# Storing the output of a macaron transformer layer from inside its last feed-forward loop, in 32 pieces, and not after it in 8

## The reference

```python
def ffn(x, U1, V1, b1, U2, V2, b2):      # 1024 -> 256 -> 4096 -> 256 -> 1024
    P = x @ U1
    H = gelu(P @ V1 + b1)
    Q = H @ U2
    return Q @ V2 + b2
def attn(x, ...):                        # 16 heads of 64, causal softmax, output projection
    ...
x = x + 0.5 * ffn(layernorm(x), U1, V1, b1, U2, V2, b2)
x = x + attn(layernorm(x), ...)
x = x + 0.5 * ffn(layernorm(x), U1, V1, b1, U2, V2, b2)
return x
```

## Time and profile before

| what | value |
|---|---|
| median of 3 runs | 2022.56 us (2018.89 to 2022.8) |
| the profiled execution, its own time | 2016.72 us |
| span of its slowest core (core 5), first to last instruction | 2015.2 us |
| spans of the eight cores | 1970.7 to 2015.2 us |
| PE busy on core 5 | 1566.1 us, 78% of the span |
| DVE, ACT busy | 28%, 28% |
| DMA traffic | 72.69 MB, mean 36 GB/s |
| granted clock of PE on core 5 | 0.752 of full speed on average |

### The profile page before, as it was taken

The page is one execution under the profiler, slowest core; times in us unless marked ns, Lnnn a source line. Parts: engine busy times, 40 slices in busy tenths (PEclk is TensorE's granted clock), DMA queues, the critical chain, the costliest instruction groups (busy, mean ns, idle before and its releaser), DMA issues. The chain is left out here.

```text
span 2015.2 us, 17883 instructions; the slowest of 8 cores (1970.7 to 2015.2 us)
## 1 busy us (share of the span) xinstructions
PE 1566.1 (78%) x5640; PEld 417.8 (21%) x5640; DVE 566.7 (28%) x947; ACT 557.2 (28%) x615; POOL 105.6 (5%) x117
## 2 busy tenths in 40 slices
PE   2389999547659879697797986969878794799994
PEld 0022222112212112121121221212211230222220
DVE  2522211752321413314133141231411236221111
ACT  1232232200013333333333333333444103222320
POOL 0100000000000001000010000100000101000000
PEclk7598899769866858678585685876865895878976
DMA  8400000300130010200102001010000125000004
GB/s 249 128 0 0 1 0 1 105 21 32 32 73 1 11 43 0 53 1 11 42 1 53 1 11 43 0 42 1 0 22 0 52 61 180 1 0 0 1 0 167
DMA packets 70984, 72.69 MB, mean 36 GB/s; under 512 B 20551, under 2 KB 59607, under 8 KB 68846
## 3 DMA queue, kind: packets, MB, share of 16 engines
q1 hardware_dynamic: 70894, 71.54, 12.4%
HBM read 50.49 MB, written 12.58 MB: 31 GB/s over the span
## 5 line engine op out<-in xcount | busy, mean ns | idle before, releaser
L725 ACT ACTIVATE pt<-p_big 128x1024 bf16<-128x1024 f32 (+3 forms) x320 | 286.5, 895 | 584.6 <-PE p_big L686 328.4
L680 PE MATMUL p_big<-qgA,kgA 65*128 65x512 bf16 (+3 forms) x320 | 147.5, 461 | 128.5 <-ACT pt L725 67.8
L570 ACT ACTIVATE hb<-p_big 128x1024 bf16<-128x1024 f32 x128 | 130.9, 1024 | 329.4 <-PE p_big L493 325.1
L491 PE MATMUL p_big<-pb,v1b 128*128 128x512 bf16 x512 | 164.8, 406 | 15.7 <-DVE pb L528 15.7
L639 PE MATMUL p_big<-pt,v_pair 128*64 128x512 bf16 (+3 forms) x320 | 155.3, 485 | 0.0
L642 PE MATMUL p_big<-pt,v_pair 128*64 128x512 bf16 (+3 forms) x320 | 154.6, 483 | 0.0
L686 PE MATMUL p_big<-qgB,kgB 65*128 65x512 bf16 (+3 forms) x320 | 153.8, 481 | 0.0
L635 PE MATMUL p_big<-pt,ones_bf 128*1 128x512 bf16 (+3 forms) x320 | 152.2, 476 | 0.0
L631 PE MATMUL p_big<-pt,ones_bf 128*1 128x512 bf16 (+3 forms) x320 | 143.9, 450 | 0.3
L501 PE MATMUL p_big<-hb,u2b 128*128 128x512 bf16 x512 | 139.3, 397 | 4.7 <-ACT hb L570 4.7
L230 PE MATMUL p_big<-xb_s,ones_bf 128*1 128x512 bf16 x96 | 50.8, 529 | 77.0 <-DVE xb_s L251 76.8
(11 more groups left out here) (149 smaller groups left out, 1604.2 us busy)
## 6 DMA issues: line engine op xcount, KB each, us to landing
wstage<-u SPq DMA_DIRECT2D x40, 256.0 KB, 4.9
wstage<-v SPq DMA_DIRECT2D x40, 256.0 KB, 4.5
x<-xT SPq DMA_DIRECT2D x8, 1024.0 KB, 11.1
outT<-x SPq DMA_DIRECT2D x8, 1024.0 KB, 10.2
wstage<-vw SPq DMA_DIRECT2D x16, 256.0 KB
vscr<-vb_s SPq DMA_DIRECT2D x32, 128.0 KB
v_pair<-vscr SPq DMA_DIRECT2D x8, 512.0 KB
wst<-ow SPq DMA_DIRECT2D x8, 512.0 KB, 4.2
```

The costliest lines, as they stand in the source:

```text
L491: tensor.matmul(psl, v1b[:, rc, 128 * fc:128 * (fc + 1)], pb[:, c % 2, rc, :], start=(rc == 0), stop=False)
L570: ACT.inc(scalar.activation(hb[:, 2 * (fp % 2):2 * (fp % 2) + 2, :], psl.rearrange("p (a b) -> p a b", a=2), AF.Gelu_apprx_tanh))
L680: mm = tensor.matmul(p_big[:, 0:w], kgA[:, ksl], qgA[:, lo:hi], start=True, stop=not first)
L725: ch["XA"].inc(scalar.activation(pt[:, :, i % 2, 0:w], p_big[:, 0:1024].rearrange("p (a b) -> p a b", a=2)[:, :, 0:w], AF.Exp))
```

## The change

The stores move into the main block of `f2`. SP gets a stream there: for each chunk and each `xadd` it waits until VectorE has done that `xadd`, and issues two DMAs, one for each feature block, of 128 partitions by 512 tokens (256 KB; 2 KB for each partition, to rows of `outT` that are 8 KB apart). The eight stores of 1 MB after the block are gone. In their place stands a block in which ScalarE waits for the semaphore of all stores. The sublayer `f1` is built as before.

```diff
                     pos = {ev: fp0 + i + 1 for i, ev in enumerate(plan)}
                     dpos = {ev: ws0 + i + 1 for i, ev in enumerate(dplan)}
+
+                    if tag == "f2":
+                        @blk.sync
+                        def _(sync):
+                            for c in range(NTC):
+                                for dp in range(4):
+                                    sync.wait_ge(EV.h, dpos[("xadd", c, dp)])
+                                    for f in (2 * dp, 2 * dp + 1):
+                                        ST.inc(sync.dma_start(
+                                            d_out.ap()[128 * f:128 * (f + 1),
+                                                       512 * c:512 * (c + 1)],
+                                            x[:, f, 512 * c:512 * (c + 1)]), 16)
...
         if PHASES >= 3:
             emit_ffn_sublayer("f2")
 
-        emit_dump_fm(d_out, x)
+        with nc.Block() as blk:
+            @blk.scalar
+            def _(scalar):
+                scalar.wait_ge(ST.h, ST.v)
```

## The result

| | before | after |
|---|---|---|
| median, 16 runs each | 2019.19 us (2011.54 to 2028.86) | 1996.51 us (1981.5 to 2021.99) |
| ratio | | 0.9878, 95% interval 0.9855 to 0.9901 |
| profiled execution | 2016.72 us | 2000.59 us |
| behind the last addition, slowest core | 22.0 us | 3.1 us |

The change made the kernel faster by 1.2%, 20 to 29 us by the interval. The direction is as forecast.

A forecast was written before the change was run, and what follows sets the result against it. The kernel was taken to end in a 22.0 us tail of output stores behind one wait. Shrinking it moves the span from 2015.2 to 1996.4 us; 2022.56 - 18.8 gives 2003.8 us, range 1997 to 2010.5.

The forecast's parts named there:

- The kernel's end is a pure transfer behind the last addition: After f2's last addition no engine computes for 22.0 us; 8.39 MB of stores take 20.1 of them at 419 GB/s.
- The stores of chunks 0 to 2: 24 DMAs, 6.3 MB, hidden in f2's main block: cost 0 on the path, 15.0 us out of the tail.
- The stores of chunk 3: Eight DMAs near f2's end: three of four pairs land before the last addition ends; the last pair's bytes take 1.5 us.
- The new tail: From the last addition's end at 1993.2 through issue, first byte, bytes and landing to the span's end at 1996.4 us.
- The upper bound: Last pair at the end: landing 4.9 us after the second issue, as 256 KB loads did; end 1998.9, gain 16.3 us.
- the sum: End of kernel: 1993.2 + 0.1 + 0.7 + 1.5 + 0.6 + 0.3 = 1996.4 us, a gain of 18.8 us.
- Cores that end together: Final stores overlapping a neighbour core's land 1.9 us later; without that overlap the gain is up to 20.7 us.
- From the span to the median: Whole kernel: the 18.8 us gain taken off the median of the runs, 2022.56, gives 2003.8 us.
- Pieces one at a time: Rival, chunk 3's eight stores: each 256 KB finishes before the next moves, 2.6 us each; time 2008.8; chance 0.07.
- Fetch held up: Rival, f2's main block: PE's instruction fetches wait behind store bursts, 14.4 us lost, time up to 2018; chance 0.05.
- The clock gives it back: Rival, f2: DMA bursts keep PE's granted clock at 0.50 longer; time 2010 to 2036 us; chance 0.04.
- No effect: Rival: SP cannot issue before the block ends, all bytes stay in the tail; 2022.6 us or slightly more; chance 0.04.

The follow-up runs named there:

- again: The changed kernel measured again without any edit, beside runs of the kernel before: 1990.39 us against 2013.88, ratio 0.9892.

## Why the prediction was right or wrong

*The kernel's end is a pure transfer behind the last addition.* Right. With the stores at the end restored the time was back (0.9997), and the changed kernel's tail is 3.1 us.

*The stores of chunks 0 to 2 cost nothing on the path.* Right, as far as the runs resolve it. The main block of f2 lasts 249.4 us with and without them, and leaving 30 of the 32 stores out changed nothing beyond the noise of 5 us.

*The stores of chunk 3: 1.25 to 1.77 us for a pair, 1.5 taken.* The runs show 382 GB/s, 1.4 us. Right.

*The new tail, 3.2 us; bounds 2.9 and 5.7.* It was 3.1. The upper bound, taken from loads that queue behind others, was far off for the last pair: its second piece was issued at 1996.4 and had landed at 1998.8, 2.4 us later (of all 32 stores half land in 2.1 to 2.3 us, the slowest in 4.5). The fixed cost of 2.0 us that the prediction takes from the Trainium skill, page "DMA: Bandwidth & Descriptors", section "Anatomy of one DMA — SWDGE (gpsimd) path", is measured there on DMAs issued from GpSimd, and these are issued from SP, so that its coming within 0.2 us of the sum is no support for either. Going below the 1 MiB of that page's "Rules for kernel authors" cost little in queued stores: 382 against 419 GB/s.

*Cores that end together: up to 1.9 us more.* Mis-sized. Cores 6 and 7 of the one profile were 8 us apart, so they overlapped only in part. At 1.3 us apart the cost is 3 to 4 us (25.5 to 26.0 against 22.3), and the last pairs of two neighbours can still meet after the change (3.9 and 3.8 us in again). I gave it as a bound for the gain and left it out of the middle; the mean tail of the eight cores before, 22.5 against the 22.0 of the slowest, already held half a microsecond of it.

*From the span to the median: "The likeliest time is 2022.56 - 18.8".* This is the step that failed. The base was the median of three runs. Sixteen gave 2019.19, and four later measurements on three chips gave 2011.5 to 2015.1. That is 3.4 of the 7.3 us. The other 3.9 are the gain, 22.7 us measured against 18.8. Of these 0.1 is the sum's own error and a part, between 0.5 and 4 us, the neighbours. What then remains lies within the error of the medians: the mean over the eight cores fell by 19.9 (17.5 to 22.4). I had taken the scatter of the executions from three runs and one profile as 3.9 to 5.8 us; over 16 runs before it is 17 us, and the range's low end was drawn from the smaller number. That the median came out only 0.5 us below it says little either way.

Whether a few microseconds of true gain stand behind the four ratios beyond tail and neighbours stays open. No block of f2 shows them, but the mean over the cores doesn't follow the tails everywhere: it lies 5 us lower than they say in the kernel with stores in f2 and at the end, and 4.6 us lower with chunk 3 at the end, both beyond two standard errors of the means, though the tails are read from one profile each. That is an effect of a size like the one sought, and it is unexplained.

*The rivals.* Pieces one at a time: excluded by the 32 pieces at the end (24.0 us of tail, not 83) and by the 7.4 us tail of chunk 3. Fetch held up: the lengths of the block exclude it. The clock gives it back: the 4.28 and 7.71 us groups stand, and the clock in f2 is 0.84, 0.89 or 0.93 with or without stores. No effect: excluded.

## What to carry to other kernels

A result that stays on the chip until the end and is final in parts long before can be stored part by part behind compute that leaves the DMA engines idle: what is left of the tail is one piece, here 3.1 us of 22. The tail of such a change can be worked out from one profile to a tenth of a microsecond, but the time of the slowest of eight cores is a draw: take the base from many executions, or compare the mean over the cores. After the transfer is gone, look at what is now last; here it was a turn-taking over PSUM banks worth 7.5 to 7.8 us, and since f1 and f2 come from one function, its removal paid twice. Before a surplus is put down to scatter, check in how many places the edit acts.

## What the runs showed that I had not expected

Stores of 256 KB with rows of 2 KB reach 382 GB/s, 91% of those of 1 MB with 8 KB rows (419), where loads with 2 KB rows in this kernel move 278. The main block of a feed-forward sublayer doesn't vary freely from core to core: its lengths cluster (249.4, 258.2, 261.5 and 262.3 us are the commonest, then 250.2, 259.4 and 273.1), and cores of different kernels share them to a tenth; the longer the block, the lower its mean granted clock (0.93, 0.89 and 0.84 at 249, 261 and 273 us). Two neighbours that store 8.4 MB at the same time need up to 26.0 us each in eight stores and 28.2 in 32, where one that stores alone needs 22.0 and 24.0.
